# A two-layer gated cross-attention block with routed experts: AV products in pairs, V projection per group in 32-column tiles

## The reference, cut to what matters

```
x = x + tanh(g[0]) * attention0(layernorm(x), ctx, mask)   # 16 heads of 8, softmax over 64 keys
x = x + tanh(g[1]) * ffn0(layernorm(x))                    # top 1 of 8 experts, 128 -> 512 -> 128, gelu
x = x + tanh(g[2]) * attention1(layernorm(x), ctx)         # 16 heads of 8, no mask
x = x + tanh(g[3]) * ffn1(layernorm(x))                    # top 2 of 16 experts, capacity 8 per sequence
# inside an attention, per sequence and head:
scores = q @ k.T ; probs = softmax(scores / sqrt(8)) ; out = probs @ v
```

## Time and profile before

| what | value |
|---|---|
| three runs | 522.56, 524.49 and 531.90 us; the median is 524.49 us |
| profiled execution, first to last instruction (its span) | 522.8 us |
| the profiled execution's own time | only its span is given; it stands 1.7 us below the median and 0.2 us above the lowest run |
| mean granted TensorE clock | 0.968 of full speed |
| attention 0 / experts 0 / attention 1 / experts 1, roughly | 17 to 172 / 180 to 274 / 283 to 437 / 437 to 522 us |

### The profile page before, as it was taken

How to read it: one execution, slowest core, us unless ns; L and a number is a source line. 1 busy time by engine, 2 the same in 40 slices (tenths; PEclk the granted TensorE clock), 3 DMA queues, 4 the chain that set the end, 5 groups by cost and what they waited for, 6 DMA issues and landing times.

```text
span 522.8 us, 22052 instructions
## 1 busy us (share of the span) xinstructions
PE 446.0 (85%) x8481; PEld 325.6 (62%) x8481; DVE 367.3 (70%) x977; ACT 321.4 (61%) x764; POOL 273.2 (52%) x325
## 2 busy tenths in 40 slices
PE   2788899799978795999999689997897787889996
PEld 1455676566756585999984466665665565545554
DVE  5678788979787766355542779989898787544555
ACT  2355576566755773677754566767767467675653
POOL 2622534655474358888886435453444326534454
PEclk9999999999999988899999899999999999598999
DMA  7123444242111144665445010110031000000112
GB/s 204 50 55 114 109 124 122 61 113 69 45 39 37 40 98 104 89 94 73 48 37 153 2 43 5 43 34 23 3 84 35 21 4 3 2 1 6 41 51 68
DMA packets 50630, 30.69 MB, mean 59 GB/s; under 512 B 12384, under 2 KB 46944, under 8 KB 50528
## 3 DMA queue, kind: packets, MB, share of 16 engines
q1 hardware_dynamic: 37072, 18.54, 13.4%
q0 software_dynamic: 6640, 4.67, 7.0%
q10 hardware_dynamic: 6816, 6.07, 4.3%
HBM read 19.41 MB, written 9.85 MB: 56 GB/s over the span
## 4 chain that ended last, share of the span: by engine, by line
PE 45%; DVE 21%; issue 16%; POOL 7%; ACT 4%; DMA 3%; ACTq 1%; DVEq 1%; SPq 0%; POOLq 0%
DVE maxes L604 8%; PE T_ps L871 6%; PE S_ps L860 6%; POOL x_mid L1153 5%; PE A_ps L886 4%; PE m_H_ps L1464 3%; PE S_ps L854 2%; PE m_X_ps L1491 2%; PE m_T_ps L1504 2%; DVE prob L612 2%; PE f_H_ps L1205 2%; PE Q_ps L753 2%; PE Q_ps L841 2%; PE m_X_ps L1475 2%; PE m_X_ps L1447 2%
## 5 line engine op out<-in xcount | busy, mean ns | idle before, releaser
L604 DVE TENSOR_REDUCE maxes<-S_ps 128x8 f32<-128x512 f32 x128 | 87.5, 684 | 40.6 <-PE S_ps L860 40.6
L431 POOL TENSOR_TENSOR k_blk<-kT,col_a 128x512 f32<-128x512 f32 x64 | 67.9, 1070 | 82.1 <-ACT kT L492 57.9
L534 ACT ACTIVATE probT<-T_ps 128x512 f32<-128x512 f32 x128 | 76.1, 595 | 46.8 <-PE T_ps L871 46.0
L612 DVE TENSOR_TENSOR prob<-S_ps,maxes 128x512 f32<-128x512 f32 x128 | 88.5, 691 | 4.4
L871 PE MATMUL T_ps<-col_a,prob 128*128 128x128 f32 x512 | 83.1, 285 | 9.0 <-DVE prob L612 5.2
L871 PEld LDWEIGHTS T_ps<-col_a,prob 128*128 128x128 f32 x512 | 56.7, 143 | 46.9 <-issue 34.4
L1153 POOL DMA_INDIRECT x_mid<-f_out,f_rows x39 | 60.9, 1562 | 11.9 <-issue 10.7
L860 PE MATMUL S_ps<-k_blk,qT 32*64 32x256 f32 x1024 | 46.6, 411 | 5.3 <-DVE prob L612 4.5
L1018 DVE TENSOR_TENSOR f_hid<-f_H_ps,f_b 128x512 f32<-128x512 f32 x39 | 26.9, 691 | 33.3 <-PE f_Y_ps L1219 27.9
L886 PE MATMUL A_ps<-v_blk,probT 128*32 128x18 f32 x4096 | 48.4, 187 | 0.4 <-issue 0.4
L886 PEld LDWEIGHTS A_ps<-v_blk,probT 128*32 128x32 f32 x4096 | 41.8, 110 | 9.7 <-issue 8.9
(11 more groups left out here) (202 smaller groups left out, 881.2 us busy)
## 6 DMA issues: line engine op xcount, KB each, us to landing
f_w<-in_W ACTq DMA_DIRECT2D x16, 256.0 KB, 2.8
ctxT<-in_ctxT SPq DMA_DIRECT2D x12, 256.0 KB, 3.1
f_rows<-sorted_rows SPq DMA_DIRECT2D x39, 64.5 KB, 2.0
out<-m_final SPq DMA_DIRECT2D x32, 64.0 KB, 1.5
x_all<-in_x SPq DMA_DIRECT2D x6, 256.0 KB, 5.7
x_mid<-x_all SPq DMA_DIRECT2D x6, 256.0 KB
x_all<-x_mid SPq DMA_DIRECT2D x6, 256.0 KB, 3.6
ctxT<-in_ctxT SPq DMA_DIRECT2D x8, 128.0 KB, 3.1
```

Source lines behind the costliest of these rows:

```text
L431: nc.gpsimd.tensor_tensor(k_blk[:, t % 2, :, :, :], kT[:, g.at(R), t - g.first, :].rearrange("p (b k) -> p b k", b=2).unsqueeze(2).to_broa ...
L534: nc.scalar.activation(probT[:, t % 2, 4 * h:4 * h + 4, :], T_ps[:, :, :], ACT.Exp, scale=SCALE).then_inc(probT_ready, 1)
L604: nc.vector.tensor_reduce(maxes[:, t % 2, h, :, :], half_of(h), X, ALU.max).then_inc(max_ready, 1)
L612: nc.vector.tensor_tensor(prob[:, t % 2, heads, :].rearrange("p (r e) k -> p r e k", r=2), half_of(h), maxes[:, t % 2, h, :, :].unsqueeze( ...
```

## The change

What it does:

- `attend` runs for both tiles of a pair in one slot: for tiles f and f+1 in slot f+2 (`pair_end`). `probT` gets a third buffer (`PR = 3`), and ACT's wait for a free one moves with it.
- V is projected for a whole group in the slot of its first tile, behind `attend` and `logit` and ahead of `turn_av` and `project_q`. A product now has 32 keys as its stationary side (array tiles of 128 by 32) and still 64 columns to stream, so that there are 16 products for two tiles in place of 8.
- ACT copies V of a group out in two copies (64 partitions by 512 elements for four tiles), at the same slot. The semaphores `v_made` and `v_ready` count groups and no longer units.
- The buffers `m1_silu` and `m1_hid` of the last stage move to another place of SBUF, which makes room for the third `probT`.

The core of the diff:

```diff
+def pair_end(skew):
+    return lambda t: t // 2 * 2 + 1 + skew
...
+    PR = 3
...
-    probT = sb("probT", [P, 2, HP, P])
+    probT = sb("probT", [P, PR, HP, P])
...
-        def v_ahead(u):
-            return NT + 3 + 2 * u.group.own + u.k
+        def v_ahead(g):
+            return NT + 3 + 2 * g.own
...
-            def v_out(u):
-                g, at = u.group, slice(2 * u.k, 2 * u.k + u.n)
-                act.wait_ge(v_made, u.i + 1)
+            def v_out(g):
+                act.wait_ge(v_made, g.i + 1)
                 act.wait_ge(zeroed, 3)
                 wait(act, av_made, tiles_to(g.i - R))
                 for s in range(2):
                     half = slice(s * S, (s + 1) * S)
-                    last = nc.scalar.copy(v_blk[half, g.at(R), at, ...
+                    last = nc.scalar.copy(v_blk[half, g.at(R), 0:g.n, ...
...
-                    wait(act, av_made, t - 1)
-                    nc.scalar.activation(probT[:, t % 2, 4 * h:4 * h + 4, :], T_ps[:, :, :], ACT.Exp, ...
+                    wait(act, av_made, t + 1 - PR)
+                    nc.scalar.activation(probT[:, t % PR, 4 * h:4 * h + 4, :], T_ps[:, :, :], ACT.Exp, ...
...
-            steps = [..., (keep_logits, ...), (avT_out, groups, tail(2)), (q_out, groups, head(-2)),
-                     (v_out, late_units, unit_head(-1)), (k_out, late, head(-3)),
+            steps = [..., (keep_logits, ...), (v_out, late_v, head(0)), (avT_out, groups, tail(2)), (q_out, groups, head(-2)),
+                     (k_out, late, head(-3)),
...
-            def project_v(u):
+            def project_v(g):
...
-                bank.take(v_ready, u.i + 1)
-                for k in range(2 * u.k, 2 * u.k + u.n):
+                bank.take(v_ready, g.i + 1)
+                for k in range(g.n):
                     for b in range(2):
-                        for s in range(2):
-                            last = nc.tensor.matmul(V_ps[s * S:(s + 1) * S, k, b, :, :], ctxT[:, g.at(CR), k, b * S:(b + 1) * S],
-                                                    wv[:, :, s, :], start=True, stop=True, skip_group_check=True)
+                        for c in range(P // QUARTER):
+                            keys = slice(b * S + c % 2 * QUARTER, b * S + (c % 2 + 1) * QUARTER)
+                            last = nc.tensor.matmul(V_ps[c * QUARTER:(c + 1) * QUARTER, k, b, :, :], ctxT[:, g.at(CR), k, keys],
+                                                    wv[:, :, c // 2, :], start=True, stop=True, skip_group_check=True,
+                                                    tile_position=(0, c * QUARTER))
...
-                     (rank ...), (attend, tiles, shift(1)), (logit, groups[:7], ...),
+                     (rank ...), (attend, tiles, pair_end(1)), (logit, groups[:7], ...), (project_v, late_v, head(0)),
                      (turn_av, groups, tail(2)), (project_q, groups, head(-2)), (output, groups, tail(3)),
                      (logit, groups[7:], settled(6, 9, short, later)),
-                     (project_v, late_units, unit_head(-1)), (project_k, late, head(-3)),
+                     (project_k, late, head(-3)),
...
-    silu = space.take("m1_silu", [P, 2, N])
-    hid = space.take("m1_hid", [P, 2, N])
+    silu = late.take("m1_silu", [P, 2, N])
+    hid = late.take("m1_hid", [P, 2, N])
```

More of the change, by code:

```diff
@@ L328, in of @@
         late = [g for g in groups if g not in early]
-        early_units = [u for g in early[:2] for u in g.units]
-        late_units = [u for u in units if u not in early_units]
+        early_v = early[:2]
+        late_v = [g for g in groups if g not in early_v]
         main, ahead = Programs(), Programs()
@@ L397, in load_ctx @@
                     sp.wait_ge(k_made, g.i - CR + 1)
-                    sp.wait_ge(v_made, units_to(g.i - CR))
+                    sp.wait_ge(v_made, g.i - CR + 1)
                 sp.dma_start(ctxT[:, g.at(CR), 0:g.n, :],
@@ L500, in v_out @@
                     half = slice(s * S, (s + 1) * S)
-                    last = nc.scalar.copy(v_blk[half, g.at(R), at, :, :, 2 + s * DK:2 + (s + 1) * DK].rearrange("p u b j d -> p (u b j) d"),
-                                          V_ps[half, at, :, :, :].rearrange("p u b j d -> p (u b j) d"))
+                    last = nc.scalar.copy(v_blk[half, g.at(R), 0:g.n, :, :, 2 + s * DK:2 + (s + 1) * DK].rearrange("p u b j d -> p (u b j) d"),
+                                          V_ps[half, 0:g.n, :, :, :].rearrange("p u b j d -> p (u b j) d"))
                 last.then_inc(v_ready, 1)
@@ L508, in scalar_ahead @@
             k_out, v_out = scalar_steps(act)
-            return [(k_out, early, k_ahead), (v_out, early_units, v_ahead)]
+            return [(k_out, early, k_ahead), (v_out, early_v, v_ahead)]
         def scalar(act):
@@ L532, in step @@
                     act.wait_ge(probs_turned, 2 * t + h + 1)
-                    wait(act, av_made, t - 1)
-                    nc.scalar.activation(probT[:, t % 2, 4 * h:4 * h + 4, :], T_ps[:, :, :], ACT.Exp, scale=SCALE).then_inc(probT_ready, 1)
+                    wait(act, av_made, t + 1 - PR)
+                    nc.scalar.activation(probT[:, t % PR, 4 * h:4 * h + 4, :], T_ps[:, :, :], ACT.Exp, scale=SCALE).then_inc(probT_ready, 1)
                 return step
@@ L590, in scalar @@
             k_out, v_out = scalar_steps(act)
-            steps = [(exp(1), tiles, shift(0)), (keep_ranks, groups, settled(7 if masked else 8, 12, short, later)), (keep_logits, groups, settled(6, 9, short, later)), (avT_out, groups, tail(2)), (q_out, groups, head(-2)),
-                     (v_out, late_units, unit_head(-1)), (k_out, late, head(-3)),
+            steps = [(exp(1), tiles, shift(0)), (keep_ranks, groups, settled(7 if masked else 8, 12, short, later)), (keep_logits, groups, settled(6, 9, short, later)), (v_out, late_v, head(0)), (avT_out, groups, tail(2)), (q_out, groups, head(-2)),
+                     (k_out, late, head(-3)),
                      (exp(0), tiles, shift(-1)), (r_xnT_out, groups, settled(5, 8, short, later)), (xnT_out, groups, turn_x_at), (normed, tiles, normed_at), (r_normed, units, lambda u: settled(4, 7, short, later)(u.group))]
@@ L753, in project_k @@
                 nc.tensor.matmul(Q_ps[:, 0:g.n, :], w["wk"][:, :], ctxT[:, g.at(CR), 0:g.n, :], start=True, stop=True).then_inc(k_made, 1)
-            def project_v(u):
-                g = u.group
+            def project_v(g):
                 wv = w["wv"][:, :].rearrange("p (j r d) -> p j r d", j=HP, r=2)
@@ L778, in stream @@
                 stream_into(S_ps[1][:, 0, :].rearrange("p (u k) -> p u k", k=P), Q)
-            return [(project_k, early, k_ahead), (stream, early, k_ahead), (project_v, early_units, v_ahead), (stream, early_units, v_ahead),
+            return [(project_k, early, k_ahead), (stream, early, k_ahead), (project_v, early_v, v_ahead), (stream, early_v, v_ahead),
                     (stream, range(STREAMED), lambda n: 2 * NT)]
@@ L878, in attend @@
                 m = (t - u.first) * HP
-                pe.wait_ge(v_ready, u.i + 1)
+                pe.wait_ge(v_ready, g.i + 1)
                 wait(pe, divided, u.i)
@@ L885, in attend @@
                         queries = slice(c * part, (c + 1) * part)
-                        last = nc.tensor.matmul(AV[queries, m + j, :], probT[:, t % 2, j, queries],
+                        last = nc.tensor.matmul(AV[queries, m + j, :], probT[:, t % PR, j, queries],
                                                 v_blk[:, g.at(R), t - g.first, c * part // S, j, :], start=True, stop=True,
@@ L909, in tensor @@
             steps = [score_ahead] + awake + [(turn_probs(1), tiles, shift(0)),
-                     (rank if masked else rank_slots, groups, settled(7 if masked else 8, 12, short, later)), (attend, tiles, shift(1)), (logit, groups[:7], settled(6, 9, short, later)),
+                     (rank if masked else rank_slots, groups, settled(7 if masked else 8, 12, short, later)), (attend, tiles, pair_end(1)), (logit, groups[:7], settled(6, 9, short, later)), (project_v, late_v, head(0)),
                      (turn_av, groups, tail(2)), (project_q, groups, head(-2)), (output, groups, tail(3)),
                      (logit, groups[7:], settled(6, 9, short, later)),
-                     (project_v, late_units, unit_head(-1)), (project_k, late, head(-3)),
+                     (project_k, late, head(-3)),
                      (turn_probs(0), tiles, shift(-1)), (turn_r, groups, settled(5, 8, short, later)), (turn_x, groups, turn_x_at)]
```

## The result

The changed kernel takes 584.31 us (median of 4 runs, 579.14 to 589.44) against 526.67 us before (4 runs, 522.56 to 531.90): 1.109 times as long, 95% interval 1.100 to 1.119. I had forecast 528.8 us in a range of 515 to 537. The time is far outside, and the forecast is wrong. In some executions of any kernel here the granted clock is lower and the time longer; ratios and intervals leave those out.

A forecast was written before the change was run, and what follows sets the result against it. The prediction took a PE-DVE handshake in the attention slots as the bound, with PE's excess work paid. It summed 4.8 + 3.5 - 1.7 - 2.3 = +4.3 us, to 528.8 us on the median, range 515 to 537.

The forecast's parts named there:

- How a slot's length comes about: Attention slots: the later of score plus 2.75 us of DVE, and PE's other work, of which about 1.85 us are free.
- balance: Attention slots: full ones pay for added PE work, light ones gain little from work removed; net +4.3 us.
- AV in pairs, PE's own time: AV runs on PE: pairing saves 0.16 us of tiling switches per pair, 5.1 us less PE work over 32 pairs.
- V of a group: V on PE: 0.97 us for four tiles in place of 2 x 0.63; all V work falls by 4.2 us.
- slots f+2: Third tile's slot in each group of four, 12 slots: a second AV adds 0.60 us to full slots; sum +4.8 us.
- slot f: First tile's slot in each group of four, 12 slots: PE gets +0.95 us, mostly hidden by DVE's late work; sum +3.5 us.
- f+1: Second tile's slot in each group of four: loses an AV, 0.76 us, which pays in five slots; sum -1.7 us.
- f+3: Fourth tile's slot in each group of four: loses AV and V, 1.3 us, but has room or waits for DVE; 0.
- That PE's saved work arrives whole: Rival for the attention stages: PE's saved 9.3 us all shorten the time, 515.2 us; chance 0.20.
- Covered slots: Rival: DVE's late work hides the additions in slots f and f+2, so -4.0 us, 520.5 us; chance 0.22.
- Column tiles one after another: Rival for V on PE: column tiles don't run side by side, 1.9 us for four tiles, 540 us; chance 0.08.

The follow-up runs named there:

- e5: The changed kernel with 32 tiny products (128 records of PE) put ahead of its work: 581.26 us, ratio 1.104.
- e3: The changed kernel with AV on array tiles of 64 columns, so half as many records in a pair: 575.09 us, against 523.99 for the kernel before.

## Why the prediction was wrong, point by point

**How a slot's length comes about: right.** PE's work beyond 1.85 us is paid (slots 18 and 40 above). The direction was right too, but for a part of the reason only: of the 46.5 us below, 13 are balance.

**AV in pairs, PE's own time: right.** At full clock and without a gap 128 records start to start take 1.19 to 1.31 us; two times 0.60 and 0.07 was the forecast.

**V of a group: right in what it costs PE, wrong in what was left out.** A run of four tiles takes 1.03 to 1.10 us to the next, where it isn't stopped; the forecast was 1.04 with its exit. The median of the twelve runs is 2.9 us. The step that failed is the one that took AV's spacing of 8.9 ns, and 0.60 us for a second AV, as a rate that PE can hold for any length: the supply of instructions has no term in the sum, so it stood at nothing. The runs showed 24 us for it in the attention stages. Rows of the trace before already showed otherwise, logits that stop after 29 of 32 records with "issue" as the reason:

```profile
102.02 0.42 PE L814 MATMUL X_ps<-col_b,r_xnT 128*32 128x8 f32 x29
104.14 0.23 PE L814 MATMUL X_ps<-col_b,r_xnT 128*32 128x8 f32 x3 [1.70 <-issue]
```

The prediction doesn't mention that gap and has no rival for it.

**The clock: left out.** The prediction reads the clock as granted in full before, and its sum takes that over to the changed kernel without a reason. Half-clock stretches between first and last scores went from 3.4 to 30.7 us, and cost about 9 us. They also explain why PE's busy time rose: the same matmul is counted for longer, as Q's 1.87 us in slot 10.

**The sum.** In the attention stages gaps take 27.9 us after (the one between AV and Q included) and 4.0 before: 24 of the 46.5 us that were lost. Read slot by slot, without gaps: the 21 even slots at full clock grew by 19.2 us and the 28 odd ones shrank by 13.8 us; the 13 slots with a stretch of half clock, nine of them even, grew by 17.1 us. An even slot costs 0.91 us by balance, so nine of these are 8 us, the balance is 19.2 - 13.8 + 8 = 13 us, and the clock about 9 us. The forecast had 4.3 us for the balance, a third of it.

By kind of slot, without gaps: slots f+2 were right, 4.8 us in the ten at full clock (forecast 4.8 in all twelve). The term that was mis-sized is slot f: the forecast let DVE's late work hide most of the 0.95 us and had 3.5 us in all, and the seven at full clock grew by 7.2 us, 1.03 each, which makes an estimated 12 us for twelve. A part came back in the slots behind: f+1 shrank by 6.6 us (forecast 1.7) and f+3 by 4.1 in the nine at full clock (forecast 0). A slot f and the one behind it together grew by 0.76 us in those seven places, where the forecast has 0.15. That DVE's late work hid a delay in one slot only to give up the cover in the next is my reading of this; no run tests it.

The remaining 8 us of the span lie outside these stages, and 6 of them behind the last score. Two of the 19 gaps stand there, in the AV of the last tiles, with 3.1 us. In the last stage 20.5 and 3.4 us ran at half clock, against 13.7 and 3.4 before; I didn't test what that costs.

**The rivals.** That PE's saved work arrives whole: refuted. Covered slots: refuted, full slots did grow. Column tiles one after another: refuted by V's 1.03 us. What happened was none of them. The 25 ns between matmuls of the Trainium skill (TensorE: Matmul & The Clock Gate, "Wait — 56ns, not 53.3ns?") doesn't hold here either: V's 64 records take 1.03 us where nothing stops them, 16 ns each.

## What to carry to other kernels

A run of small matmuls is limited by how fast instructions come in, not only by array time: count the instructions of back-to-back runs, and look for idle PE with the reason "issue" in the middle of a run, in steps of a fixed number of instructions. Spread such runs between longer matmuls, or use fewer and wider products. And where two engines alternate, work moved from a light step to a full one can be paid in full, as the 0.95 us of PE were in slots f (1.03 us each), and the idle time that it leaves may lower the clock of the step behind.

## What the runs showed of the hardware that I had not expected

- PE stops for 0.5 to 2.2 us in the changed kernel (0.3 to 2.3 in all runs) at counts of its instructions that are a multiple of 256 apart, where a fast run crosses them. Adding 128 records in front (e5) leaves the counts where they were and moves the stops to other work.
- One instruction packet of 16.4 KB keeps its DMA engine busy for about 1.0 us (2.4% of 16 engines over 2.7 us in slot 20), and PE stands for 2.15 us around it. PE goes on 1.2 to 1.6 us after such a packet is through.
- Halving the records of AV (e3) removes every gap, though a pair takes PE 0.7 us longer.
- A gap of about 2 us, or a light slot ahead of a full one, can bring the granted clock to the 1.2 GHz level; in slot 10 Q and the output then took 1.87 and 1.54 us, where they took 0.96 and 0.89 in slot 42 before.
